# Two attention blocks and a mixture of experts on one core: own orders for ramp and tail, an earlier x, other rows for the score operands, and a later residual base

## What is computed

```python
x = x + tanh(g_xattn) * xattn(layernorm(x), ctx)      # 16 heads of 8; softmax over 120 keys
h = rms(layernorm(x), n1)                             # ffn block on the normed x, M = 32
q, k, v = rms(h @ wq.T), rms(h @ wk.T), h @ wv.T      # per head
ao = softmax(causal(q @ k.T / sqrt(8))) @ v @ wo.T; ao[:, :, :M] = 0
z = layernorm(x) + ao
xf = rms(z, n2); wts = top-2 of softmax(xf @ gate.T), renormed
moe = sum_e wts[e] * expert_e(xf); moe[:, :, :M] = 0  # 4 experts of 2 to 4 layers
x = x + tanh(g_ffn) * (z + moe)
```

## Time and profile before

| | |
|---|---|
| median of 3 runs | 1121.92 us (1121.64 to 1123.22) |
| profiled execution | 1120.12 us |
| its span | 1118.4 us, mean granted TensorE clock 0.982 |
| busy: TensorE, weight load | 1010.6 us (90%), 622.6 us (56%) |
| busy: VectorE, ScalarE, POOL | 806.0 (72%), 734.0 (66%), 334.9 us (30%) |
| DMA | 114.26 MB, mean 102 GB/s |

### The profile page before, as it was taken

How to read it: one execution, slowest core, us unless ns; L and a number is a source line. 1 busy time by engine, 2 the same in 40 slices (tenths; PEclk the granted TensorE clock), 3 DMA queues, 4 the chain that set the end, 5 groups by cost and what they waited for, 6 DMA issues and landing times.

```text
span 1118.4 us, 25981 instructions
## 1 busy us (share of the span) xinstructions
PE 1010.6 (90%) x8578; PEld 622.6 (56%) x8578; DVE 806.0 (72%) x2170; ACT 734.0 (66%) x1331; POOL 334.9 (30%) x458
## 2 busy tenths in 40 slices
PE   3657799999999999999999999999999999998897
PEld 1334456656565655656565565655565565555454
DVE  7457777777877777787778777787777778655423
ACT  3455667676776766677676667768676767765453
POOL 6422314051422414151331405142241415132120
PEclk9979899999999999999999999999999999999899
DMA  6426533454433334454333344443333444403100
GB/s 193 111 48 185 142 94 71 117 126 123 126 104 98 101 85 111 123 126 123 100 102 87 87 122 126 123 121 102 97 92 89 125 123 112 118 9 93 33 10 10
DMA packets 77156, 114.26 MB, mean 102 GB/s; under 512 B 7616, under 2 KB 40000, under 8 KB 76992
## 3 DMA queue, kind: packets, MB, share of 16 engines
q1 hardware_dynamic: 76752, 111.54, 38.2%
q10 hardware_dynamic: 368, 2.24, 0.6%
HBM read 58.97 MB, written 53.74 MB: 101 GB/s over the span
## 4 chain that ended last, share of the span: by engine, by line
PE 56%; DVE 23%; ACT 10%; issue 8%; DMA 2%; POOL 0%; DVEq 0%; SPq 0%; ACTq 0%; POOLq 0%
PE ps_pv L1161 9%; PE ps_w L1187 7%; PE ps_s2a L1140 6%; PE ps_s2a L1198 5%; PE ps_s2b L1140 4%; PE ps_s2b L1205 4%; ACT probs L787 4%; DVE mpadB L915 4%; PE ps_t L1044 4%; DVE mpadA L915 3%; PE ps_w L1205 3%; PE ps_t L1174 2%; PE ps_w L1122 2%; PE ps_w L1118 2%; DVE ym L944 2%
## 5 line engine op out<-in xcount | busy, mean ns | idle before, releaser
L787 ACT ACTIVATE probs<-ps_s2a 120x512 f32<-120x512 f32 (+1 forms) x256 | 153.7, 600 | 92.3 <-PE ps_s2a L1140 86.8
L915 DVE TENSOR_REDUCE mpadB<-ps_w 128x4 f32<-128x512 f32 x256 | 158.6, 682 | 29.0 <-PE ps_w L1122 29.0
L915 DVE TENSOR_REDUCE mpadA<-ps_w 128x4 f32<-128x480 f32 x252 | 147.8, 649 | 36.7 <-PE ps_w L1122 36.6
L787 ACT ACTIVATE probs<-ps_s2b 120x512 f32<-120x512 f32 (+1 forms) x256 | 154.0, 602 | 0.0
L678 POOL TENSOR_SCALAR_AFFINE_SELECT probs<-probs 128x1024 f32<-128x1024 f32 x128 | 139.8, 1092 | 0.1
L1187 PE MATMUL ps_w<-W,hid 128*128 128x96 f32 x1024 | 130.0, 281 | 4.4 <-DVE split_k L821 1.1
L1187 PEld LDWEIGHTS ps_w<-W,hid 128*128 128x128 f32 x1024 | 122.2, 195 | 16.4 <-issue 13.5
L649 POOL TENSOR_TENSOR rB<-vrB,neg_half 128x4 f32<-128x4 f32 x16 | 16.1, 1007 | 374.1 <-DVE veB L814 374.1
L1140 PE MATMUL ps_s2a<-qdA,kstA 128*120 128x512 f32 x128 | 69.3, 541 | 14.9 <-issue 7.9
L944 DVE SCALAR_TENSOR_TENSOR ym<-ps_w,gates,ym 128x96 f32<-128x96 f32 x192 | 47.6, 310 | 43.6 <-PE ps_w L1187 43.5
L1198 PE MATMUL ps_s2a<-hid,W 128*128 128x512 f32 x160 | 78.4, 604 | 0.0
(11 more groups left out here) (202 smaller groups left out, 2086.4 us busy)
## 6 DMA issues: line engine op xcount, KB each, us to landing
scratch_Aq<-split_q SPq DMA_DIRECT2D x48, 256.0 KB, 2.4
qdA<-scratch_Aq SPq DMA_DIRECT2D x64, 192.0 KB
scratch_Bq<-split_q SPq DMA_DIRECT2D x48, 256.0 KB, 2.4
scratch_Bk<-split_k SPq DMA_DIRECT2D x48, 256.0 KB, 3.0
qdB<-scratch_Bq SPq DMA_DIRECT2D x64, 192.0 KB
kstB<-scratch_Bk SPq DMA_DIRECT2D x64, 192.0 KB
scratch_Ak<-split_k SPq DMA_DIRECT2D x48, 240.0 KB, 2.3
kstA<-scratch_Ak SPq DMA_DIRECT2D x64, 180.0 KB
```

Of the source, the lines that this page charges most:

```text
L787: nc.scalar.activation(probs[0:k, slot_of(part, *index), :], bank[0:k, :], ACT.Exp, scale=SCALE if part == "A" else 1.0).then_inc(done, 1)
L915: nc.vector.tensor_reduce(mneg[OP[part]][:, :, c, b], bank[:, 0:HT * k].rearrange("p (h k) -> p h k", h=HT), AX.X, ALU.max, negate=True).t ...
```

## The change

- Stack j lies on partitions j, j+4, ... 92 (`slice(j, M_ROW, HT)`), and the maxima in partition 96.
- "load" is split in "load" (x) and "ctx". The first x and context are issued ahead of all steps; in the ramp the next x goes out in the step before (in the first one after norm and base). ctx has own waits.
- All four ramp steps and the first three tail steps have own orders (`fourth_group`, `last_queries`, `last_self_keys` are new); own banks are only handed out where a use has another ring than in SCHEDULE.
- "base" stands at the step's end and waits for kd_ready of the same group.
- In the last step down(1) waits for fewer banks, and e2_l2 waits for the others.

```diff
@@ -111,7 +111,7 @@
 
 def self_attention():
 
-    return (one("N", "load", 0, None) + exact("D", 0, 0) + one("B", "hT") + down(1) + exact("D", 0, 2)
+    return (one("N", "load", 0, None) + one("N", "ctx", 0, None) + exact("D", 0, 0) + one("B", "hT") + down(1) + exact("D", 0, 2)
             + one("B", "qk", 0) + one("B", "qk", 1) + one("B", "qk", 2) + one("B", "qk", 3)
             + exact("D", 1, 0) + estimate("A", 0) + exact("D", 1, 2)
             + one("B", "squares", 0, None) + values("D", 0)
@@ -147,9 +147,10 @@
     return (fill("D", "e1_w1", 0, "w") + one("A", "wo", 0, "t") + fill("D", "e1_w2", 0, "w") + values("A", 3)
             + one("D", "gates", 0, None) + fill("D", "e1_w1", 1) + one("A", "oT", 1, "t") + fill("D", "e1_w2", 1)
             + one("A", "nT", 1, "t") + estimate("B", 3) + fill("D", "e2_l1", 0) + one("A", "wo", 1, "t") + one("A", "stats", 0, None)
-            + one("N", "base", 0, None) + fill("D", "e2_l1", 1) + fill("D", "e3_down", 0) + one("D", "gates", 1, None)
+            + fill("D", "e2_l1", 1) + fill("D", "e3_down", 0) + one("D", "gates", 1, None)
             + one("B", "mT") + one("N", "q") + one("D", "gates", 2, None) + one("A", "norm", 0, None) + one("N", "v") + one("N", "k")
-            + fill("D", "e0_up", 0) + fill("D", "e0_up", 1, "w") + one("D", "gates", 3, None))
+            + fill("D", "e0_up", 0) + fill("D", "e0_up", 1, "w") + one("D", "gates", 3, None)
+            + one("N", "base", 0, None))
 
 def slot_of(part, b, c):
@@ -167,56 +168,103 @@
 
 def first_group():
 
-    return (one("N", "load", 0, None) + one("N", "stats", 0, None) + one("N", "norm", 0, None) + one("N", "base", 0, None)
+    return (one("N", "stats", 0, None) + one("N", "norm", 0, None) + one("N", "base", 0, None) + one("N", "load", 0, None)
             + one("N", "xT") + one("N", "q", 0, "f") + one("N", "k", 0, "f") + one("N", "v", 0, "pv")
-            + estimate("A", 0) + estimate("A", 1, "ffww") + estimate("A", 2, "wwff") + estimate("A", 3) + one("A", "mT"))
+            + estimate("A", 0) + estimate("A", 1, "ffww") + estimate("A", 2, "wwff") + estimate("A", 3) + one("A", "mT")
+            + one("N", "ctx", 0, None))
 
 def second_group():
 
...
+    return (one("N", "stats", 0, None) + one("N", "norm", 0, None)
+            + exact("A", 0, 0) + exact("A", 0, 2) + one("N", "xT") + exact("A", 1, 0) + one("N", "q") + exact("A", 1, 2) + one("N", "k")
+            + values("A", 0) + exact("A", 2, 0) + estimate("A", 0) + exact("A", 2, 2) + values("A", 1)
+            + exact("A", 3, 0) + one("A", "oT", 0, "t") + estimate("A", 1) + exact("A", 3, 2) + values("A", 2)
+            + one("A", "nT", 0, "t") + estimate("A", 2) + values("A", 3) + one("A", "oT", 1) + one("A", "wo", 0, "t") + one("N", "v")
+            + one("A", "nT", 1, "t") + estimate("A", 3) + one("A", "wo", 1, "t") + one("A", "stats", 0, None)
+            + one("A", "mT") + one("A", "norm", 0, None)
+            + one("N", "base", 0, None) + one("N", "ctx", 0, None) + one("N", "load", 0, None))
 
 def third_group():
 
...
+    return (exact("A", 0, 0) + exact("A", 0, 2) + exact("A", 1, 0) + exact("A", 1, 2) + one("B", "hT") + values("A", 0)
+            + one("B", "qk", 0) + one("B", "qk", 1) + one("B", "qk", 2) + one("B", "qk", 3)
+            + exact("A", 2, 0) + one("B", "squares", 0, None) + exact("A", 2, 2) + values("A", 1)
+            + exact("A", 3, 0) + one("A", "oT", 0, "t") + exact("A", 3, 2) + one("B", "sums", 0, None) + one("B", "root", 0, None)
+            + values("A", 2) + one("B", "init", 0, None) + one("B", "copy", 0, None) + one("A", "nT", 0, "t") + one("B", "scale", 0, None)
+            + values("A", 3) + one("A", "wo", 0, "t") + one("N", "stats", 0, None) + one("A", "oT", 1) + one("B", "v")
+            + one("B", "qT") + one("B", "kT") + one("N", "norm", 0, None) + one("A", "nT", 1, "t")
+            + estimate("B", 0) + one("A", "wo", 1, "t") + one("N", "xT") + estimate("B", 1) + one("N", "q") + estimate("B", 2)
+            + one("N", "k") + estimate("B", 3) + one("A", "stats", 0, None) + one("N", "v")
+            + one("B", "mT") + one("A", "norm", 0, None) + one("N", "base", 0, None))
+
+
+def fourth_group():
+
+    return (one("N", "load", 0, None) + one("N", "ctx", 0, None) + exact("D", 0, 0) + one("B", "hT") + exact("D", 0, 2)
+            + one("B", "qk", 0) + one("B", "qk", 1) + one("B", "qk", 2) + one("B", "qk", 3) + estimate("A", 0)
+            + exact("D", 1, 0) + exact("D", 1, 2) + estimate("A", 1) + one("B", "squares", 0, None) + values("D", 0)
+            + exact("D", 2, 0) + exact("D", 2, 2) + estimate("A", 2) + values("D", 1) + one("B", "sums", 0, None)
+            + exact("D", 3, 0) + one("D", "oT", 0, "t") + exact("D", 3, 2) + estimate("A", 3) + values("D", 2)
+            + one("D", "nT", 0, "t") + one("B", "root", 0, None) + one("A", "mT") + values("D", 3) + one("D", "wo", 0, "t")
+            + one("B", "scale", 0, None) + one("D", "oT", 1) + one("N", "stats", 0, None) + one("B", "qT") + one("B", "kT")
+            + one("D", "nT", 1, "t") + one("N", "norm", 0, None) + one("D", "wo", 1, "t") + one("D", "out", 0, None)
+            + one("D", "squares", 0, None)
+            + [use for use in cross_attention() + first_experts() if use[0] in "NABD"])
+
+
+def last_queries():
+
+    order = of_parts("ABDM")
+    late = estimate("B", 3) + one("B", "mT")
+    order = [use for use in order if use not in late]
+    at = order.index(("D", "fill", ("e1_w1", 1), "f"))
+    order = order[:at] + estimate("B", 3) + order[at:]
+    at = order.index(("D", "fill", ("e2_l1", 1), "f"))
+    return order[:at] + one("B", "mT") + order[at:]
+
+
+def last_self_keys():
+
+    return (exact("D", 0, 0) + one("B", "hT") + down(1) + exact("D", 0, 2)
+            + one("B", "qk", 0) + one("B", "qk", 1) + one("B", "qk", 2) + one("B", "qk", 3)
+            + exact("D", 1, 0) + exact("D", 1, 2) + one("B", "squares", 0, None) + values("D", 0) + exact("D", 2, 0)
+            + one("B", "sums", 0, None) + exact("D", 2, 2) + one("B", "root", 0, None) + values("D", 1) + one("B", "scale", 0, None) + down(0)
+            + exact("D", 3, 0) + one("D", "oT", 0, "t") + exact("D", 3, 2) + one("B", "qT") + one("B", "kT")
+            + values("D", 2) + one("D", "nT", 0, "t")
+            + fill("M", "e2_l2", 0) + one("D", "wo", 0, "t") + estimate("B", 0) + fill("M", "e2_l2", 1)
+            + values("D", 3) + fill("M", "e3_up", 0) + one("D", "oT", 1, "t") + estimate("B", 1) + fill("M", "e3_up", 1)
+            + one("D", "nT", 1, "t") + fill("M", "e2_l3", 0) + one("D", "wo", 1, "t") + one("D", "out", 0, None) + estimate("B", 2)
+            + fill("M", "e2_l3", 1) + estimate("B", 3) + one("D", "squares", 0, None) + down(2)
+            + one("D", "norm", 0, None) + one("B", "init", 0, None) + one("B", "copy", 0, None) + one("B", "mT")
+            + down(3) + one("M", "store", 0, None) + one("D", "xfT") + one("B", "v") + one("D", "logits")
+            + fill("D", "e1_w1", 0, "w") + fill("D", "e1_w2", 0, "w") + fill("D", "e1_w1", 1, "w") + fill("D", "e1_w2", 1, "w")
+            + fill("D", "e2_l1", 0) + fill("D", "e2_l1", 1) + fill("D", "e3_down", 0, "w")
+            + fill("D", "e0_up", 0, "w") + fill("D", "e0_up", 1, "w")
+            + one("D", "gates", 0, None) + one("D", "gates", 1, None) + one("D", "gates", 2, None) + one("D", "gates", 3, None))
 
 def last_self_values():
 
...
 
 def last_experts():
 
-    return (down(1) + fill("M", "e2_l2", 0) + fill("M", "e2_l2", 1) + down(0) + fill("M", "e2_l3", 0) + fill("M", "e2_l3", 1, "w")
-            + fill("M", "e3_up", 0) + fill("M", "e3_up", 1) + down(2) + down(3) + one("M", "store", 0, None))
+    return (down(1) + fill("M", "e2_l2", 0) + fill("M", "e2_l2", 1) + down(0) + fill("M", "e2_l3", 0) + fill("M", "e2_l3", 1)
+            + fill("M", "e3_up", 0, "w") + fill("M", "e3_up", 1, "w") + down(2) + down(3) + one("M", "store", 0, None))
 
 def bank_of_each_use(order):
@@ -230,7 +278,7 @@
 
 def banks_of(order):
 
-    own = [use for use in SCHEDULE if use in order] != order
+    own = any(use not in SCHEDULE for use in order)
     return bank_of_each_use(order if own else SCHEDULE)
 
@@ -247,18 +295,18 @@
 
 PARTS = "NABDM"
 
-AHEAD = {"s1": (-1, 0), "mT": (-1, 0)}
-RAMP = [(-1, "N", first_group()), (0, "NA", second_group()), (1, "NAB", third_group()), (2, "NABD", of_parts("NABD"))]
+AHEAD = {("A", "s1"): (-1, 0), ("A", "mT"): (-1, 0), ("N", "load"): (-1, 0), ("N", "ctx"): (-1, 0)}
+RAMP = [(-1, "N", first_group()), (0, "NA", second_group()), (1, "NAB", third_group()), (2, "NABD", fourth_group())]
 LOOP = (3, NG - 1)
-TAIL = [(NG - 1, "ABDM", of_parts("ABDM")), (NG, "BDM", of_parts("BDM")), (NG + 1, "DM", last_self_values()), (NG + 2, "M", last_experts())]
+TAIL = [(NG - 1, "ABDM", last_queries()), (NG, "BDM", last_self_keys()), (NG + 1, "DM", last_self_values()), (NG + 2, "M", last_experts())]
 
 def expected(t, parts):
 
     def present(part, work):
```

(51 more changed lines are left out.)

39 lines of the change are left out of this document (11 added, 28 removed).

## The result

The changed kernel is slower: 1137.72 us (median of 4, 1134.74 to 1139.58) against 1122.33 for the kernel before on the same chip, ratio 1.0134 (95% interval 1.0109 to 1.0159). The forecast was 1105 with a range of 1095 to 1113. The profiled execution took 1138.83 us, its span is 1137.1, the mean granted clock 0.954.

What follows compares the result with a forecast made beforehand. TensorE sets the steady step's pace (busy 61.5 of 64.1 us); ramp and tail idle or run at the lower clock. -2.8 - 1.3 + 0.0 - 1.2 - 10.0 - 1.5 = -16.8, so 1103.3 profiled, 1105 median, range 1095 to 1113.

Steps and rivals of the forecast that it cites:

- (d): Rival, chance 0.04: pauses at hT and qk merge, the clock falls in every looped seam, +26 us, 1131.
- Part 1: Start of step 0: the row of maxima lands earlier, first score matmul at 30.4 instead of 34.6, 4.1 us gained.
- Part 2: Step 0 (second_group): 28.6 us instead of 33.0, the middle between bounds; step 1 starts at 59.0 instead of 67.6.
- Part 3: Step 1 (third_group): a loss of 10.5 us, bounds +3 to +13; step 2 starts at 105.3 instead of 103.3.
- Part 4: Step 2 (fourth_group): cross estimates moved to the front save 4.8 us; ramp total -2.8.
- Part 5: Seam between steps: 0.85 us gained at hT, given back at fourth qk; 0.0 for 12 looped seams, -1.3 into the first.
- Part 6: Tail: step 15 -1.2 us, step 16 (last_self_keys) -10.0, steps 17 and 18 -1.5 (+1 to -4).

Runs made afterwards that it cites:

- a1: The kernel before with only the score operands on alternating partitions: 1119.46 us, ratio 0.998.
- a4: The kernel before with only the new ramp (early x, ctT's own use, three new lists), contiguous rows and old base: 1140.05 us, ratio 1.0157.
- d1: c4 with the old order of step 2: 1100.70 us, ratio 0.9814.
- c4: The changed kernel with old step 1 order, POOL's copy of the kept columns ahead of the base, old lists and waits of steps 17 and 18: 1101.35 us.
- d2: c4 with the stacks on contiguous rows again: 1103.22 us, ratio 0.982.
- d3: The changed kernel with old step 1 order, POOL's copy ahead of the base, step 17's down(1) and down(0) one score-matmul pair earlier: 1103.01 us.
- e1: d1 with the old order of step 0 also, leaving only the early loads of the new ramp: 1103.46 us, ratio 0.9829.
- d4: The kernel before with alternating rows, base behind the key factors, POOL's copy ahead of it, new lists of steps 15 and 16, old ramp: 1096.60 us.

## Why the prediction was wrong

The forecast was a gain of 16.8 us, and the kernel lost 15.4. Of the 35.5 us between forecast and profiled time the ramp has 18.5, the looped steps 7.2 and the tail 9.8. The only rival that was slower, (d), had a chance of 0.04 and named the clock alone.

**Part 1 was right in size, wrong in part.** 31.06 instead of 30.4: the row of maxima, issued at 27.84, landed in 3.1. But with the rows alone a1 starts at 32.4, with the early x alone a4 at 33.6: the early x gives 1.0 where I had 3.3 for it, and the layout 2.2 where I had 0.8. In a4 the row takes 5.4 us to land, as the stack loads are still moving at 152 GB/s from 30 to 32 us. From 24 to 28 us the DMA engines moved 222 GB/s in the changed kernel, against 164 in the kernel before and in a4. By the ports and the rate of each in the Trainium skill (SBUF — State Buffer, "Door 1: The DMA port swizzle"), 16 instead of 6 would more than double the rate, an estimate from its figures, where the prediction has near to doubling; the trace agrees in the direction, with a third more. So the prediction's 163 beside 170 does not show that the ports set the old rate.

**Part 2 failed:** 33.2 for the forecast 28.6. I took the middle between two bounds, a gain of 4.4, and the order is worth 0.5 to 1.8 in these traces; only a4 came near (29.8). In part it is what the earlier start meets: POOL's causal factor stands at a fixed time and takes up to 1.7 us from VectorE's key factors, while I costed the step as if it moved as a whole. What makes up the rest stays open.

**Part 3 had the sign and the places, not the size:** +17.6 for +10.5. Key factors end 25.6 us into the step against 17.7 before: +7.9 for the forecast +6.2. From there to the issue of the row it is 24.4 against 15.3, +9.1 for the forecast +3.8. The estimates with q and k between them stand in a row of waits:
```profile
99.71 0.61 PE L1176 MATMUL ps_w<-causal_k,causal_q 32*128 32x512 bf16 x4 [2.23 <-DVE split_q L879]
...
101.59 1.94 PE L1122 MATMUL ps_w<-ctT,W 96*128 96x480 f32 x2 [0.84 <-DVE mpadB L973]
...
106.15 0.61 PE L1176 MATMUL ps_w<-causal_k,causal_q 32*128 32x512 bf16 x4 [2.61 <-DVE split_k L879]
...
117.61 0.76 PE L1198 MATMUL ps_s2a<-qdB,kstB 128*128 128x512 f32 x1 [7.34 <-issue]
```
Each estimate waits for a bank until the q or k in front of it has gone through matmul, ScalarE and VectorE: a serial round of some 6.4 us, where I had counted VectorE's instructions alone and half of those hidden. With these waits the clock stands at 0.50 for 30.7 us from 90.8 on, so the matmuls of the round double as well. And SP holds the row for 3.4 us instead of 2.5.

The slow issue of the strided loads is not what costs here. a4 has contiguous rows and the same list (SP, then TensorE):
```profile
108.55 1.84 SPq L553 DMA_DIRECT2D kstA<-scratch_Ak  x4
110.45 0.47 SPq L602 DMA_DIRECT2D qdB<-mTB  x1
```
```profile
119.56 0.77 PE L1195 MATMUL ps_s2a<-qdB,kstB 128*128 128x512 f32 x1 [10.37 <-issue]
```
There the row is ready at 109.81 and held for 0.6 us only, but it lands 9.0 us after its issue, behind the same eight loads, which move at 168 GB/s; step 1 takes 56.2. In the changed kernel it lands in 3.25. So the cost is the place behind the loads, for which the sum had 2.5 and 0.5: 6.7 us from ready to first matmul in the changed kernel, 9.8 in a4, 2.8 before.

**Part 4 failed:** +1.3 instead of -4.8. The root of self-attention ended 19.8 us into the step (forecast 17, and 16.3 in the old order), and the cast of kT at 26.9 (forecast 22.8, before 26.6). I had counted ScalarE's work up to the root, with the estimates' maxima beside it. But VectorE takes the scale up only 1.8 us behind the root, after an instruction that waited 2.1 us for a transpose, and TensorE does the transposes of qk in 1.97 us at half clock, for 1.04 in the loop. The table load before the cross scores came at 27.7, where it was 27.2 before. The new list saves nothing here: d1, with the old one, has 57.5 for c4's 58.4.

**Part 5** was right to the tenth in mechanism (0.9 gained, 0.03 left), and so was the first looped step (-1.8 for -1.3), with some luck: d2 and d3, whose seams have no merged wait, keep its clock fall and take 66.8 and 66.2. What failed is rival (d)'s threshold: I let it decide from 2 us idle within a seam, since one seam had shown that; with a single wait of 1.33 it came in 4 of 12 steps, +1.4 each. Another 0.2 us in each step comes with the early loads (e1 against d4), in small losses of TensorE of 0.06 to 0.09 at three fixed places; the new lists of steps 0 and 2 are ruled out by e1 and d1. The looped step issues the same instructions in both, and what causes the losses no run tells.

**Part 6:** step 16 gained 8.4 for 10.0, with the clock at 0.97, the strongest of the steps foretold. Step 15 gained nothing of 1.2. Steps 17 and 18 lost 5.5 where I had given a gain of 1.5 with an upper end of +4: I had read its new order for banks and chains, and not asked, as in part 3, what is queued behind a matmul whose bank isn't drained. Of the loss in steps 17 and 18, 0.9 to 3.1 go with down's place (d3), the rest with other parts of the two lists.

Three errors of one kind, then: in parts 3, 4 and 6 a list was costed by each engine's work, and what cost the time was the fixed order on TensorE, VectorE and SP behind one waiting instruction. Part 2 was a middle taken between bounds, with no step of the work behind it.

## What to carry to other kernels

Where engines walk one written list, cost a new order by asking for each instruction that can wait what ready work stands behind it; four score matmuls ahead of ready ones held them up for 2.2 us here, and eight loads ahead of one row cost it 4.0 us from ready to first matmul with the rows spread and 7.0 without. Ask it of the transfers too: an earlier issue did not bring the row in earlier, as the loads ahead of it were still moving. Moving a wait off the critical place frees its time only when what is queued behind the mover is taken along: the base alone gave 0.03 us a step, the base with POOL's copy ahead of it 1.03. And two short pauses are not one long one: in 44 looped steps of four kernels the merged wait came with 13 clock falls, in 44 with the split one there was none. Last, take several traces before a step is read: the same list in step 0 took 31.4 to 33.6 us.

## What the runs showed of the hardware

A DMA onto every fourth partition took 0.76 us of SP's queue to issue, one onto 24 neighbouring partitions 0.375, for the same bytes and packets; the loads themselves ran faster (222 against 164 GB/s from 24 to 28 us). A small DMA issued behind eight stack loads took 9.0 us to land with neighbouring partitions and 3.25 with spread ones, against 2.6 in the kernel before, where it was issued ahead of them. TensorE's clock fell in 13 of 44 looped steps of four kernels whose seam has one idle of 1.33 us, some 8 us into the step each time and for 3.4 us, and in none of 44 with idles of 0.98 and 0.31. VectorE's key factors took 1.1 to 2.8 us by how far into POOL's run of two-input multiplies they began, and ended with it.
